# A token tower on one core: the middle stage (mixer) rebuilt around 32-row strips of fp32 heads

## The reference, cut to what matters

```python
h = h + _L0_ffn_ref(_layernorm(h, axis=-1), ...)
# in _L0_ffn_ref:
h = _ln(x, ln1_g, ln1_b)
qkv = h @ in_w.T + in_b                      # 192 -> 3 * 192
q, k, v = jnp.split(qkv, 3, axis=-1)         # 12 heads of 16
scores = jnp.einsum('bqhd,bkhd->bhqk', q, k) / jnp.sqrt(jnp.float32(D))   # D = 16
attn = jax.nn.softmax(scores, axis=-1)
ctx = jnp.einsum('bhqk,bkhd->bqhd', attn, v).reshape(B, N, E)
x = x + ctx @ out_w.T + out_b
```

## Time and profile before

| | us |
|---|---|
| three runs | 1097.98, 1101.22, 1106.42; median 1101.22 |
| profiled execution | 1104.34 |
| its span in the profile | 1102.6 |
| PE, DVE, ACT, POOL busy over the span | 897.6, 610.5, 526.0, 228.3 |
| mixer, 463.8 to 761.5 us of the span | 297.7 |
| its entry, 463.8 to the first scores at 500.25 | 36.4 |
| mixer: PE, DVE, ACT, POOL busy | 210.06, 229.14, 155.12, 64.95 |
| mean TensorE clock granted there | 0.65 |

### The profile page before, as it was taken

How to read it: one execution, slowest core, us unless ns; L and a number is a source line. 1 busy time by engine, 2 the same in 40 slices (tenths; PEclk the granted TensorE clock), 3 DMA queues, 4 the chain that set the end, 5 groups by cost and what they waited for, 6 DMA issues and landing times. The chain is left out here.

```text
span 1102.6 us, 18700 instructions
## 1 busy us (share of the span) xinstructions
PE 897.6 (81%) x5796; PEld 779.1 (71%) x5796; DVE 610.5 (55%) x1588; ACT 526.0 (48%) x1432; POOL 228.3 (21%) x303
## 2 busy tenths in 40 slices
PE   0069999999999999538568688784689999999997
PEld 0058989889898988526447476572568879889786
DVE  5834244342434333168978868684435765756754
ACT  2335353544445344126426557383346555465564
POOL 6202020110202021056730000000015223241250
PEclk9999999999999999955556766777779999999999
DMA  7152233242423323233210000002010010010000
GB/s 207 68 129 69 63 74 78 60 105 55 109 59 76 78 57 101 74 99 101 63 50 18 7 21 4 11 4 71 0 34 1 1 48 0 0 48 0 15 1 15
DMA packets 48901, 57.18 MB, mean 52 GB/s; under 512 B 7456, under 2 KB 43936, under 8 KB 48864
## 3 DMA queue, kind: packets, MB, share of 16 engines
q1 hardware_dynamic: 41568, 44.20, 15.3%
q0 software_dynamic: 2368, 8.46, 2.6%
q10 hardware_dynamic: 4928, 4.07, 1.7%
HBM read 37.83 MB, written 18.87 MB: 51 GB/s over the span
## 5 line engine op out<-in xcount | busy, mean ns | idle before, releaser
L1526 DVE TENSOR_TENSOR ffn_hid_lo<-ffn_gelu,ffn_hid_hi 128x512 fp32r<-128x512 f32 x120 | 95.9, 802 | 116.0 <-ACT ffn_hid_hi L1504 106.3
L1465 PE MATMUL ffn_ps_out<-ffn_weights_w,ffn_hid_hi 128*128 128x384 f32 x480 | 146.5, 362 | 3.1 <-DVE ffn_hid_lo L1526 1.9
L1501 ACT ACTIVATE ffn_gelu<-ffn_ring,ffn_b 128x512 f32<-128x512 f32 x120 | 82.1, 684 | 125.8 <-PE ffn_ring L1454 122.9
L490 POOL TENSOR_SCALAR attn_probs<-attn_probs,attn_inverse 128x128 f32<-128x128 f32 x128 | 47.8, 373 | 358.5 <-DVE attn_inverse L713 350.7
L1466 PE MATMUL ffn_ps_out<-ffn_weights_w,ffn_hid_lo 128*128 128x192 f32 x480 | 121.3, 253 | 0.0
L1465 PEld LDWEIGHTS ffn_ps_out<-ffn_weights_w,ffn_hid_hi 128*128 128x128 f32 x480 | 90.2, 188 | 13.7 <-DVE ffn_total L1584 4.1
L1466 PEld LDWEIGHTS ffn_ps_out<-ffn_weights_w,ffn_hid_lo 128*128 128x128 f32 x480 | 91.5, 191 | 4.3
L637 ACT ACTIVATE attn_probs<-ps_scores,attn_neg_max 128x128 f32<-128x128 f32 x128 | 45.2, 365 | 82.2 <-DVE attn_neg_max L709 82.2
L1017 ACT ACTIVATE mix_probs<-mix_ps_scores,mix_neg_max 128x128 f32<-128x128 f32 x192 | 67.5, 376 | 29.9 <-DVE mix_inverse L1102 17.0
L1504 ACT ACTIVATE ffn_hid_hi<-ffn_gelu 128x512 fp32r<-128x512 f32 x120 | 75.9, 632 | 3.8
L720 DVE COPY attn_mixed_rows<-ps_pairs 128x256 f32<-128x256 f32 x32 | 13.6, 425 | 88.3 <-PE ps_pairs L572 50.9
(11 more groups left out here) (299 smaller groups left out, 2661.6 us busy)
## 6 DMA issues: line engine op xcount, KB each, us to landing
v_rows<-attn_v_flat SPq DMA_DIRECT2D x16, 768.0 KB, 3.2
attn_v_rows<-v_rows SPq DMA_DIRECT2D x128, 96.0 KB, 3.3
mix_stage<-in_w POOLq DMA_DIRECT2D x5, 576.0 KB, 5.7
embed_stage_main<-in_w_qkv SPq DMA_DIRECT2D x3, 768.0 KB, 5.6
mix_raw_in<-in_w POOLq DMA_DIRECT2D x10, 192.0 KB, 3.1
mix_raw_in<-in_w POOLq DMA_DIRECT2D x5, 384.0 KB, 4.1
attn_xin<-h_rows ACTq DMA_DIRECT2D x8, 192.0 KB, 4.5
last_emb<-h_rows SPq DMA_DIRECT2D x8, 192.0 KB, 2.5
```

The lines of the kernel that those rows point to most:

```text
L490: last = nc.gpsimd.tensor_scalar(probs[:, n, j, :], probs[:, n, j, :], inverse[:, n, j:j + 1], float(D) ** -0.5, ALU.mult, ALU.mult)
L1465: nc.tensor.matmul(ps_out[:, b, 0:2 * D], hid_hi[:, i % 3, tile], w2[:, c, :, :], start=c == 0, stop=False)
L1501: nc.scalar.activation(gelu[:, i % 2, :], ring[:, bank(slot), :], ACT.Gelu, bias=b1[:, f * HC + c:f * HC + c + 1]).then_inc(chunk_read.sem, 1)
L1526: nc.vector.tensor_tensor(hid_lo[:, i % 3, :], gelu[:, i % 2, :], raw(hid_hi[:, i % 3, :]), ALU.subtract).then_inc(lo_ready.sem, 1)
```

## The change

`mixer` is written anew; the order is now one list in Python, written out for all 16 tiles without a loop. A tile t has steps S(t), M(t), and T, A and O of tile t-1 stand between them: `S(t) T(t-1) M(t) A(t-1) ... O(t-1)`. Q and k are plain fp32 now. Eight heads of 16 sit in pairs in four groups of 32 rows; a group holds three heads (`SETS`), and k is masked by `even` and `odd` rows, so that a product over 32 rows gives one head. The whole tile's maximum is taken in two pieces and is the bias of the exponential; the scale 1/4 is put into q. The row sums come from a product with a matrix of ones. The output of P.V is already turned, so that the transposes back go.

```diff
@@ attention
+            for b in range(UNIT):
+                sp.wait_ge(h1_stored[b].sem, h1_stored[b].at(UNITS - 2, 0))
+            sp.dma_start(keep["hin"][:, 0:EARLY, :], dram["h1"][0:EARLY * P, :]...).then_inc(keep["hin_loaded"], 16)
             body(UNITS - 1, False)
@@ attention, gpsimd, ahead of its loop
+            for part, (to, of) in enumerate(...3 pieces...):
+                pool.dma_start(mix_raw[to, min(part, 1), :], dram["w_mix"][of, :]).then_inc(mix_loaded, 16)
+            pool.wait_ge(mix_loaded, 48)
+            nc.gpsimd.tensor_scalar(mix_hi[:, :], mix_raw[:, 0, :], 1.0, 1.0, ALU.mult, ALU.mult)
+            nc.gpsimd.tensor_scalar(mix_half[:, :], mix_raw[:, 1, :], keep["low_rows"][:, 0:1], 1.0, ALU.mult, ALU.mult).then_inc(mix_hi_ready, 1)
+            pool.wait_ge(mix_hi_ready, 1)
+            nc.gpsimd.tensor_tensor(mix_lo[:, :], mix_raw[:, 0, :], raw(mix_hi[:, :]), ALU.subtract)
+            nc.gpsimd.tensor_tensor(mix_stack[:, :], mix_raw[:, 1, :], raw(mix_half[:, :]), ALU.subtract)
@@ mixer: the order
+        norms(0, range(NORM_PARTS))
+        projections(0, "X Q0 Q1 Q2 V0 V1 V2 V3")
+        for t in range(TILES + 1):
+            unit, j = divmod(t, UNIT)
+            if t < TILES:
+                order.append(("S", t))
+            if t:
+                order.append(("T", t - 1))
+            if t < TILES:
+                order.append(("M", t))
+            if t == 0:
+                norms(1, range(NORM_PARTS))
+            elif unit + 1 < UNITS and j == 0:
+                norms(unit + 1, range(10, NORM_PARTS))
+            if t:
+                order.append(("A", t - 1))
+            if unit + 1 < UNITS:
+                projections(unit + 1, {0: "", 1: "X Q0", 2: "Q1 Q2", 3: "V0 V1 V2 V3"}[j])
+            if unit + 2 < UNITS and j > 1:
+                norms(unit + 2, {2: range(0, 5), 3: range(5, 10)}[j])
+            if t:
+                order.append(("O", t - 1))
@@ tensor
+            def scores(t):     # waits for q, k of the unit and for exps_ready 2 * t
+                for i in range(STRIPS):
+                    rows = slice(32 * i, 32 * i + 32)
+                    nc.tensor.matmul(ps_scores[:, i, 0:2 * P], q_main[rows, ...], k_main[rows, ...], start=True, stop=True)
+                for i in range(STRIPS):
+                    last = nc.tensor.matmul(ps_scores[:, i, 2 * P:WIDE], q_tail[rows, ...], k_tail[rows, ...], start=False, stop=True, skip_group_check=True)
+                    if i % 2:
+                        last.then_inc(scored, 1)
+            def turn_probs(t):  # 12 transposes, three into each of the four banks of ring
+            def mix(t):
+                pe.wait_ge(pt_ready, STRIPS * (t + 1))
+                for s in range(SETS):
+                    for i in range(STRIPS):
+                        rows = slice(32 * i, 32 * i + 32)
+                        nc.tensor.matmul(ring[rows, bank("A", t, 0), s * P:(s + 1) * P], v_pad[:, unit % 2, b, i * SETS + s, :], pt[:, i, s, :], start=True, stop=True)
+                for i in range(STRIPS):
+                    last = nc.tensor.matmul(ring[rows, bank("A", t, 1), 0:WIDE], ones[:, :], pt[:, i, :, :]..., start=True, stop=True)
+            def project_out(t):
+                pe.wait_ge(context_ready, t + 1)
+                for s in range(SETS):
+                    last = nc.tensor.matmul(ring[:, bank("O", t), 0:D], context[:, s, :], w_out[:, s, :], start=s == 0, stop=s == SETS - 1)
@@ scalar
+                    for i in (2 * h, 2 * h + 1):
+                        for s in range(SETS):
+                            last = nc.scalar.activation(probs[:, i, s, :], ps_scores[:, i, s * P:(s + 1) * P], ACT.Exp, bias=neg_max[:, i, s:s + 1])
+            def turned_probs(t):
+                for i in range(STRIPS):
+                    act.wait_ge(turned, STRIPS * t + i + 1)
+                    nc.scalar.activation(pt[:, i, :, :], ring[:, bank("T", t, i), 0:WIDE]..., ACT.Copy).then_inc(pt_ready, 1)
@@ vector
+            def row_max(t):
+                for h in range(2):
+                    dve.wait_ge(scored, 2 * t + h + 1)
+                    nc.vector.tensor_reduce(out=neg_max[:, halves(h), :], in_=ps_scores[:, halves(h), 0:WIDE]..., op=ALU.max, axis=X, negate=True).then_inc(max_ready, 1)
+            def normalise(t):
+                dve.wait_ge(mixed, t + 1)
+                steps.then(nc.vector.reciprocal(inverse[:, :, :], by_set(1)))
+                if t:
+                    dve.wait_ge(out_filled, t)
+                nc.vector.tensor_tensor(context[:, :, :], by_set(0), inverse[:, :, :], ALU.mult).then_inc(context_ready, 1)
+            def add_out(t):
+                dve.wait_ge(out_filled, t + 1)
+                nc.vector.tensor_tensor(x2[:, t % 2, :], ring[:, bank("O", t), 0:D], hin[:, t, :], ALU.add).then_inc(out_added, 1)
```

More of the change, by code:

```diff
@@ new lines, in mixer, with norms, projections @@
+        order = []
+        def norms(unit, parts):
+            order.extend(("N", (unit, part)) for part in parts)
+        def projections(unit, steps):
+            order.extend(("X", unit) if s == "X" else (s[0], (unit, int(s[1:]))) for s in steps.split())
+        norms(0, range(NORM_PARTS))
[20 more added lines that the diff above has]
+                order.append(("O", t - 1))
@@ new lines, in mixer @@
+        slot_of, slots = {}, 0
+        for step, i in order:
+            for part in range({"X": 2, "Q": 1, "V": 1, "T": STRIPS, "A": 2, "O": 1}.get(step, 0)):
+                slot_of[step, i, part] = slots
+                slots += 1
+        bank = lambda step, i, part=0: slot_of[step, i, part] % RING
+        zt_ready, main_ready, tail_ready, v_ready = sem("zt_ready"), sem("k_main_ready"), sem("tail_ready"), sem("v_ready")
+        zt_hi_ready, q_main_ready, pt_ready = sem("zt_hi_ready"), sem("q_main_ready"), sem("pt_ready")
@@ L847, in _, with walk_order @@
+        def walk_order(do):
+            for step, i in order:
+                if step in do:
+                    do[step](i)
+        tile_of = lambda t: slice((t % UNIT) * P, (t % UNIT + 1) * P)
+        halves = lambda h: slice(2 * h, 2 * h + 2)
         @block.sync
         def _(sp):
-            def load(turn, event, unit):
-                if event == 0:
-                    sp.wait_ge(zn_ready.sem, zn_ready.at(turn, -1))
-                sp.dma_start(hin[:, :, :], dram["h1"][bass.ds(unit * UT, UT), :].rearrange("(b p) d -> p b d", p=P)).then_inc(h_loaded.sem, 16)
@@ L961, in transposes, with slot_free @@
[L961 to L969 removed]
+            def slot_free(step, i, part=0):
+                slot = slot_of[step, i, part]
+                if slot >= RING:
+                    pe.wait_ge(*emptied[slot - RING])
@@ new lines, in transposes, with project_qk @@
+            def transposes(unit):
+                pe.wait_ge(zn_ready, unit + 1)
+                for part in range(2):
+                    slot_free("X", unit, part)
+                    for b in range(UNIT):
+                        last = nc.tensor.transpose(ring[:, bank("X", unit, part), b * P:(b + 1) * P], zn[:, b, part * P:(part + 1) * P], keep["ident"][:, :])
+                    last.then_inc(x_filled, 1)
+            def project_qk(i):
+                unit, s = i
+                slot_free("Q", i)
@@ L970, in project_qk @@
                 if s == 0:
-                    pe.wait_ge(weights_ready, 1)
-                slot_free(turn, slot, source)
+                    pe.wait_ge(zt_ready, 2 * unit + 2)
                 cols = slice(s * P, (s + 1) * P)
                 passes = ((w_hi, zt_hi, 0), (w_hi, zt_lo, 0), (w_lo, zt_hi, 0), (w_stack, zt_hi, 1), (w_stack, zt_lo, 1))
-                for i, (w, z, part) in enumerate(passes):
-                    last = nc.tensor.matmul(ring[:, bank(slot), :], w[:, cols], z[:, part, :], start=i == 0, stop=i == 4)
@@ L977, in project_qk, with project_v @@
-                last.then_inc(ring_filled.sem, 1)
-            def project_v(turn, b, slot, hi, source):
-                slot_free(turn, slot)
+                for k, (w, z, part) in enumerate(passes):
+                    last = nc.tensor.matmul(ring[:, bank("Q", i), :], w[:, cols], z[:, part, :], start=k == 0, stop=k == 4)
+                last.then_inc(q_filled, 1)
+            def project_v(i):
+                unit, b = i
+                slot_free("V", i)
                 tile = slice(b * P, (b + 1) * P)
```

510 lines of the change are left out of this document (212 added, 298 removed).

## The result

Four runs of the changed kernel took 1057.01, 1059.86, 1064.14 and 1068.50 us, median **1062.0**; four of the kernel before have the median 1102.93. The ratio is 0.9635, 95% interval 0.9567 to 0.9704. The profiled execution is the lowest of the four, 1057.01, with a span of 1055.3: where a profile of another kernel is laid beside it, the changed kernel is shown at its best. A likely reason for the spread of 11 us is part of what follows.

What follows compares the result with a forecast made beforehand. The mixer was held bound by a chain going to and fro between in-order engines, DVE fullest. It would end at 726 against 761.5, gaining 36 us; attention loses 2.5: profiled 1071, median 1068 against 1101.2, range 1020 to 1108.

Steps and rivals of the forecast that it cites:

- Both rivals: Mixer's 384-column reciprocal, forecast 2.1 us: ordinary operation, 0.54 us (chance 0.22), or eight steps a column, 3.2 us (0.12).
- 7.0 + R: Mixer tile's chain at the full clock: 7.0 us plus the reciprocal, taken as 2.1, giving 9.1 us.
- the prediction's own two chains: Mixer tile's chain at each clock level: 9.1 us full, 13.5 lower; 12.2 with the clock of before, 70% low.
- I carried 0.65 over: Mixer's TensorE clock: the 0.65 granted before, low 70% of the time, was assumed for the new chain.
- the idle reciprocal as a rival that keeps the clock low: Mixer: PE idle through reciprocal and product keeps the lower clock, 21 us more, 1089; chance 0.06, counted as no change.
- Steps between: Mixer tiles: next unit's norm and projection work in the chain adds 9 us a unit, 2.3 a tile.
- A side by side: Mixer's P.V and sum products: four column groups run at once, 1.4 us; slower rival one at a time, 1145, chance 0.11.
- That goes with the split: Mixer's entry norm: 4.8 us lost by two operations behind POOL's split of the weights disappears.
- first scores near 487: Sign of being right, mixer entry: first scores start at 487 instead of 500.25.
- no 2.5 us operation in the first norm: Sign of being right, mixer entry: no operation of the first norm is stretched to 2.5 us.
- which stays as it was: Mixer: POOL's weight work is unchanged and costs 3 us for DVE behind it.
- the load of h1 by SP: Attention's end: SP's wait and loads ahead of the residual and v cost 0 to 3 us, taken as 1.

Runs made afterwards that it cites:

- e1: Changed kernel with the division left out, the sums multiplied by a constant instead of inverted: 1028.8 us, ratio 0.9316 to the kernel before.
- e7: Changed kernel plus seven unread fp32 products on PE before the output product, in the last unit and at j = 0: 1058.1 us.
- e6: Changed kernel with the three P.V products of one column group following each other instead of going round the four groups: 1076.9 us.
- e4: Changed kernel with POOL preparing the experts' weights only after the eighth tile, nothing left out: 1045.6 us, ratio 0.9469 to the kernel before.
- e5: Changed kernel with POOL's four operations that split w_mix moved from attention's entry to its end, the loads staying: 1062.7 us.

## Why the prediction was right, and where two errors met

The forecast was 1068, the time 1062, and the mechanism is the one forecast: the same chain of steps, ACT off the path, PE waiting for the context. Its terms were not all as good. Against the profiled execution the forecast was 1071 and the time 1057, 14 us apart:

| step | forecast | trace after | difference |
|---|---|---|---|
| attention | +2.5 | +3.8 | +1.3 |
| block start to first scores | 23.2 | 33.9 | +10.7 |
| S(0) to S(12), 12 turns | 173.8 | 158.3 | -15.5 |
| S(12) to the end of the last tile | 60.4 | 52.5 | -7.9 |
| POOL's work, own term | 3 | in the turns | -3 |

- **Reciprocal.** 2.56 us instead of 2.1. Both rivals fall, 0.54 and 3.2. From 4 columns (172 ns) to 384 (2557) it is 6.28 ns a column, where the two small shapes gave 5.5; the fixed part of some 150 ns in these was not in the forecast. The Trainium skill ("VectorE: DVE Perf Modes", the paragraph "Why 8 slices when ADD needs 1?") has a repeat count of 8; with the ordinary step of 1.04 ns from the rows before, the trace shows 6.0 steps a column, between that rule and the slope. e1 shows it on the path in all its length in the last unit, and in part elsewhere.
- **The chain.** At the full clock I had 7.0 + R. The turn from 585.55 to 594.71, with clock 1.00, takes 9.16: 6.6 + R. In the last unit, forecast 12.2 with the clock of before, it is 10.1 to 11.0 at clock 0.82, which by the prediction's own two chains would be 10.7.
- **The clock.** This is the main mis-sized term behind the 23 us of the two lower rows on turns: I carried 0.65 over, and the block has 0.79. By my own two chains (4.4 us apart) 28% less of the low level is 1.2 us a tile, an estimate of 20 us. The text had named the idle reciprocal as a rival that keeps the clock low. e1 and e7 show that this rival is half true: the gap does cost clock, 1.5 us a turn on average in the last unit, but not down to the lower level throughout.
- **Steps between.** 2.3 us a tile was forecast. Turns 4 to 11 average 12.73, the last unit 10.65: 2.1. This softest term held there; turn 1 is another matter (POOL, below).
- **A side by side.** 0.86 us for the products of P.V, all four column groups at once, and 1.51 for the whole of A (forecast 1.4); e6 shows that the order of issue carries it.
- **Entry.** The step "That goes with the split" failed. POOL's split went away, but not POOL: 12 us after the block's start its weight work meets the same norm, one operation further on. And two pieces of order that stand in the change were not counted, the masks ahead of the norm (3.1 us) and part 14 ahead of `zt_lo`. From the transposes X at 482.87 to S(0) it took 18.7 us, where 12 were forecast; in e4, with POOL away, the scalings of part 14 take 1.24 us instead of 7.20. The sign "first scores near 487" failed, and so did that of no 2.5 us operation in the first norm: one of these scalings took 2.66.
- **POOL.** The step "which stays as it was" failed. 3 us were taken; e4 puts what can be had back at 16.5 by the medians, of which 7.0 are at the entry and 7.0 in turn 1 by the profiles. The work is the same as before, but its operations stop DVE's where DVE stands in the chain, and hitting the third norm or not is worth 9 us from one profile to another. The mechanism of the gain is the one forecast, but that the number came within 6 us is luck: this loss and that of the entry met a clock better than assumed.
- **Attention.** All 3.8 us arise at its entry (0.5 ahead of the first statistics, 1.3 at the load of a bias, 2.1 in the scalings). From there to the end of attention it is 397.1 us, before 397.2, so the load of h1 by SP costs nothing: 1 us too many. How much of the rest is the change's is open: the mixer's block starts anywhere between 465.4 (e4) and 469.6 (e7) in kernels with this same attention, and the wait for the bias did not go with POOL's split (e5).

## What to carry to other kernels

A long operation in a chain between two engines costs its length and then what the waiting TensorE loses in clock, where nothing else fills the wait: 2.0 and 1.5 us a tile in the last unit here. Take the consumer a tile later, or start the operation earlier, before trying to shorten it. Bulk work on POOL cost nothing here beside DVE's reductions, reciprocals and statistics; beside scalings from SBUF to SBUF and chains of small operations with two inputs in SBUF it cost several times their length, and the turn depended on a phase of a few us. When an edit is costed from where a stall was seen, ask what the stalling engine does next: the stall moved on to the next operation in order.
